# A gated expert mixture on one core: the moving columns of its matrix products laid out in alternating 16-byte runs

## The chip, the core and the metric
The kernel runs on one core of one Trainium2 chip. The metric is the device time of one execution in microseconds (us), median of several. The names of the engines: PE is TensorE, the matrix engine (PEld: its weight loads), DVE is VectorE, ACT is ScalarE, POOL is GpSimd, SP is SyncE, which issues the DMAs.

## The reference, cut to what matters
`x` has 16 sequences of 128 rows and 128 columns, float32. There are 8 routed experts and a shared one, each with a gate and an up projection 128 -> 512 and a down projection 512 -> 128.

```python
g = jnp.einsum('bsd,edf->ebsf', h, Wg)
u = jnp.einsum('bsd,edf->ebsf', h, Wu)
expert_outs = jnp.einsum('ebsf,efd->ebsd', jax.nn.silu(g) * u, Wd)
expert_output = jnp.einsum('be,ebsd->bsd', gating_probs, expert_outs)
shared = jnp.einsum('bsf,fd->bsd', jax.nn.silu(h @ Sg) * (h @ Su), Sd)
x = x + (1.0 - sg) * expert_output + sg * shared
x = x + jnp.einsum('bij,bjk->bik', T[itok - 1], x)
```

## The kernel before, in words
Everything is held transposed: 128 features on the partitions, (sequence, row) pairs as columns. The 2048 columns are four x tiles of W = 512 columns (NT = 4, four sequences each); the 512 hidden features are four chunks of 128 (NC = 4). A *unit* is one expert, one x tile and one chunk: 16 units to an expert, 9 experts, N = 144 units. Per unit PE makes three products, each as three matrix products of 128x128 weights with 512 moving columns. The split in three is for precision: every float32 operand is rounded to the type fp32r (`x_hi`, `w_hi`, `h_hi`) and the remainder kept as a second such operand (`x_lo`, `w_lo`, `h_lo`); hi*hi, hi*lo and lo*hi are added up in a PSUM bank.

Nine matrix products per unit, then: `project_g` (L444 to L446, the helper `product`) into `g_bank`, `project_u` (the same lines) into one of four `u_bank`, and `project_down` of the unit two before (LAG = 2), L470, L471 and L473, into `o_bank`, summed over the four chunks. The moving operands are `x_hi`/`x_lo` tile t for g and u, and `h_hi`/`h_lo` slot k % 4 (HR = 4 slots) for down.

Around them, per unit n:
- ACT: `silu` (L278) of g_bank into silu_g, and `round_h` of unit n - 1 (L284), which writes `h_hi` from `u_bank`.
- DVE: `make_h` (L342), u_bank times silu_g in place, and `split_h` of unit n - 1 (L348), which writes `h_lo` = u_bank - h_hi. Every fourth unit also `scale_group` (L356), o_bank times the routing coefficient.
- POOL: `acc` += scaled (L260) every fourth unit, and rounding and splitting the next expert's weights (`split_chunk`, L217 and L212). Each engine has its instructions in the order of its program; the waits are semaphores. `project_down` waits for `h_rounded` ahead of L470 and for `split_done` ahead of L473; `project_g` for `g_read`; `project_u` for `split_done` of four units before.
- SP: the weights of the expert after next, three DMAs of 256 KB; later the 16 matrices T and the results.

Before the loop the x tiles are written once: tile 0 by ACT (L307, `x_hi`) and DVE (L385, `x_lo`) from `o_bank`, which stands on the way to the first products (L510, L512, L514, then `project_u(0, 0)`, and L518 for the second unit's g); tiles 1 to 3 by `round_x` on ACT (L294) and `split_x` on POOL (L233). The semaphore `acc_done` holds PE at the first unit of each x tile of the first expert until `x_lo` is there.

Behind the last expert's units come the step matrices: `turn_y` (L483, transposes) and `step_y` (L491, plain float32 products of 128 columns, eight records for four sequences), copies on ACT (L289) and DVE (L371), and the stores. Two stretches of them lie between units; the last lies at the end. Their operands aren't touched by the change.

The straight layout of before is this: `x_hi` is `[P, NT, W]`, a tile's 512 columns lie one behind the other, and a moving operand is `x_hi[:, t, :]`, likewise `h_hi[:, slot, :]`.

Of the kernel before, what the change touches and what calls it, by code (L numbers as in the profile page):

```python
# [5 lines left out]
P = 128  # L6
F32 = mybir.dt.float32
F32R = mybir.dt.float32r
# [4 lines left out]
def moe_then_step_kernel(  # L13
# [32 lines left out]
    NT = B // BT  # L46
    W = BT * S
# [7 lines left out]
    EARLY = 3  # L55
    Q = 32
    assert NC == 4 and NT == 4 and E % 2 == 0

    with ExitStack() as ctx:
# [8 lines left out]
        zero = sb("zero", [P, P])  # L68
        x_hi = sb("x_hi", [P, NT, W], F32R)
        x_lo = sb("x_lo", [P, NT, W], F32R)  # L70
        w_raw = sb("w_raw", [P, 2, NC, 3, P])
        w_hi = sb("w_hi", [P, 2, NC, 3, P], F32R)
        w_lo = sb("w_lo", [P, 2, NC, 3, P], F32R)
        silu_g = sb("silu_g", [P, 2, W])
        h_hi = sb("h_hi", [P, HR, W], F32R)
        h_lo = sb("h_lo", [P, HR, W], F32R)
        scaled = sb("scaled", [P, 2, W])
# [15 lines left out]
        u_bank = [ctx.enter_context(nc.psum_tensor(f"u_bank{i}", [P, W], F32)) for i in range(HR)]  # L93
        o_bank = [ctx.enter_context(nc.psum_tensor(f"o_bank{i}", [P, W], F32)) for i in range(2)]

        x_in = [sem(f"x_in{i}") for i in range(3)]
# [107 lines left out]
        def _(pool):  # L204
# [25 lines left out]
            def split_x(t):  # L230

                pool.wait_ge(x_rounded, t + 1)
                nc.gpsimd.tensor_tensor(x_lo[:, t, :], acc[:, t, :], x_hi[:, t, :].bitcast(F32),  # L233
                                        ALU.subtract).then_inc(acc_done, 1)
# [38 lines left out]
        def _(act):  # L273
# [6 lines left out]
            def round_h(n, k):  # L280


                act.wait_ge(h_done, n + 1)
                nc.scalar.activation(h_hi[:, k % HR, :], u_bank[k % HR][:, :], ACT.Copy).then_inc(h_rounded, 1)  # L284

# [6 lines left out]
            def round_x(t):  # L292
                act.wait_ge(x_turned, t)
                nc.scalar.activation(x_hi[:, t, :], acc[:, t, :], ACT.Copy).then_inc(x_rounded, 1)  # L294

# [10 lines left out]
            act.wait_ge(x0_turned, 1)  # L306
            nc.scalar.activation(x_hi[:, 0, :], o_bank[0][:, :], ACT.Copy).then_inc(x_rounded, 1)  # L307
            act.wait_ge(w0_in, 32)
# [28 lines left out]
        def _(dve):  # L337
# [7 lines left out]
            def split_h(n, k):  # L345

                dve.wait_ge(h_rounded, n + 1)
                nc.vector.tensor_tensor(h_lo[:, k % HR, :], u_bank[k % HR][:, :], h_hi[:, k % HR, :].bitcast(F32),  # L348
                                        ALU.subtract).then_inc(split_done, 1)
# [29 lines left out]
            for m in range(2):  # L379
# [4 lines left out]
            dve.wait_ge(x_rounded, 1)  # L384
            nc.vector.tensor_tensor(x_lo[:, 0, :], o_bank[0][:, :], x_hi[:, 0, :].bitcast(F32),  # L385
                                    ALU.subtract).then_inc(split_done, 1)
# [54 lines left out]
        def _(pe):  # L441
# [6 lines left out]
            def project_g(n, k):  # L448

                t, c = k % U // NC, k % NC  # L450

                pe.wait_ge(g_read, n - 1)
                product(g_bank[k % 2][:, :], (k // U % 2, c, 0), x_hi[:, t, :], x_lo[:, t, :],
                        True, True).then_inc(g_done, 1)

            def project_u(n, k):
                t, c = k % U // NC, k % NC
                if k >= LAG:

                    pe.wait_ge(split_done, EARLY + n + 1 - HR)  # L460
                product(u_bank[k % HR][:, :], (k // U % 2, c, 1), x_hi[:, t, :], x_lo[:, t, :],
                        True, True).then_inc(u_done, 1)

            def project_down(n, k):

                t, c, slot = k % U // NC, k % NC, k % HR
                w = (k // U % 2, c, 2)

                pe.wait_ge(h_rounded, n + 1)
                nc.tensor.matmul(o_bank[t % 2][:, :], w_hi[:, w[0], w[1], w[2], :], h_hi[:, slot, :], start=c == 0, stop=False)  # L470
                nc.tensor.matmul(o_bank[t % 2][:, :], w_lo[:, w[0], w[1], w[2], :], h_hi[:, slot, :], start=False, stop=False)  # L471
                pe.wait_ge(split_done, EARLY + n + 1)
                last = nc.tensor.matmul(o_bank[t % 2][:, :], w_hi[:, w[0], w[1], w[2], :], h_lo[:, slot, :],  # L473
                                        start=False, stop=c == NC - 1)
                if c == NC - 1:
                    last.then_inc(o_done, 1)
# [32 lines left out]
            pe.wait_ge(x_rounded, 1)  # L509
            nc.tensor.matmul(g_bank[0][:, :], w_hi[:, 0, 0, 0, :], x_hi[:, 0, :], start=True, stop=False)  # L510
            pe.wait_ge(split_done, 1)
            nc.tensor.matmul(g_bank[0][:, :], w_lo[:, 0, 0, 0, :], x_hi[:, 0, :], start=False, stop=False)  # L512
            pe.wait_ge(split_done, EARLY)
            nc.tensor.matmul(g_bank[0][:, :], w_hi[:, 0, 0, 0, :], x_lo[:, 0, :], start=False, stop=True).then_inc(g_done, 1)  # L514
            project_u(0, 0)

            pe.wait_ge(w_ready, 1)
            product(g_bank[1][:, :], (0, 1, 0), x_hi[:, 0, :], x_lo[:, 0, :], True, True).then_inc(g_done, 1)  # L518
            project_u(1, 1)
# [58 lines left out]
```

## Time and profile before

| | us |
|---|---|
| time, median of 2 runs | 311.86 (311.65 to 312.06) |
| the profiled execution's own time | 312.09 |
| its span, first to last instruction | 310.1 |
| PE busy | 305.5 (99% of the span) |
| DVE busy | 217.5 (70%) |
| ACT busy | 164.6 (53%) |
| POOL busy | 102.2 (33%) |

The profile is that of one execution. A group of instructions is one line of the kernel with its operation, the tiles it writes and reads, and its shape; behind the count stand the busy time, the mean of one in ns, and the idle time of its engine just before, with what ended it. Matrix products are pipelined: a product's listed duration reaches past the start of the next, so rates are read from start to start. Start times are us from the span's start.

### The profile page before, as it was taken

To read this page: it belongs to the slowest core of one execution; us is meant where nothing else is said; L and a number is where in the kernel's file an instruction comes from. 1 tells how busy PE (TensorE), PEld (TensorE's weight loads), DVE (VectorE), ACT (ScalarE), POOL (GpSimd) and SP (SyncE) were. 2 spreads that over 40 slices of the span, in tenths; PEclk is the share of its full clock that TensorE was granted. 3 is DMA by queue.
4 is the path that set the end of the run, shared out by engine and by line. 5 is a ranking of instruction groups with operands and counts; after the bars stand their busy time and mean duration, and the time that the engine had idled before them with its cause. 6 is when DMAs were issued, how large, how long until landed. Compare 5 with 4: busy or idle time off the path is not lost.

```text
span 310.1 us, 4762 instructions
## 1 busy us (share of the span) xinstructions
PE 305.5 (99%) x1364; PEld 253.3 (82%) x1364; DVE 217.5 (70%) x355; ACT 164.6 (53%) x306; POOL 102.2 (33%) x116
## 2 busy tenths in 40 slices
PE   8999999999999999999999999999999999999996
PEld 7688888888888888888888888888888888888885
DVE  2786667766676666776667766677666766668885
ACT  5565555555555555555555555555555555555552
POOL 2565312441155115511552134411441155111310
PEclk9999999999999999999999999999999999999999
DMA  6930300030001100030003001100013000000112
GB/s 159 201 89 2 103 1 2 0 94 7 1 0 45 56 0 0 0 101 0 0 0 109 13 13 17 17 14 13 15 17 110 0 0 0 0 2 0 34 36 68
DMA packets 32727, 10.39 MB, mean 34 GB/s; under 512 B 16208, under 2 KB 32720, under 8 KB 32720
## 3 DMA queue, kind: packets, MB, share of 16 engines
q1 hardware_dynamic: 32720, 10.30, 13.5%
q8 instruction: 4, 0.07, 0.1%
q14 instruction: 3, 0.02, 0.0%
HBM read 9.25 MB, written 1.05 MB: 33 GB/s over the span
## 4 chain that ended last, share of the span: by engine, by line
PE 95%; SPq 1%; DMA 1%; POOL 0%; DVE 0%; ACT 0%; issue 0%
PE o_bank L470 11%; PE o_bank L473 11%; PE o_bank L471 11%; PE g_bank L446 10%; PE u_bank L446 10%; PE g_bank L445 10%; PE u_bank L445 10%; PE g_bank L444 10%; PE u_bank L444 10%; DMA w_raw<-in_L_cond_Wd 1%; PE o_bank L491 1%; SPq L158 1%; PE o_bank L483 0%; POOL w_lo L212 0%; DVE res L371 0%; PE u_bank L483 0%
## 5 line engine op out<-in xcount | busy, mean ns | idle before, releaser
L342 DVE TENSOR_TENSOR u_bank<-u_bank,silu_g 128x512 f32<-128x512 f32 x144 | 100.7, 699 | 84.2 <-PE u_bank L446 82.6
L278 ACT ACTIVATE silu_g<-g_bank 128x512 f32<-128x512 f32 x144 | 86.1, 598 | 132.8 <-PE g_bank L446 132.4
L348 DVE TENSOR_TENSOR h_lo<-u_bank,h_hi 128x512 fp32r<-128x512 f32 x144 | 97.9, 680 | 0.1
L260 POOL TENSOR_TENSOR acc<-acc,scaled 128x512 f32<-128x512 f32 x32 | 41.5, 1296 | 163.2 <-DVE scaled L356 163.0
L284 ACT ACTIVATE h_hi<-u_bank 128x512 fp32r<-128x512 f32 x144 | 85.4, 593 | 0.7 <-DVE u_bank L342 0.7
L470 PE MATMUL o_bank<-h_hi,w_hi 128*128 128x512 f32 x144 | 56.2, 390 | 0.8 <-POOL w_lo L212 0.8
L444 PE MATMUL u_bank<-x_hi,w_hi 128*128 128x512 f32 x144 | 56.1, 390 | 0.0
L473 PE MATMUL o_bank<-h_lo,w_hi 128*128 128x512 f32 x144 | 56.0, 389 | 0.0
L445 PE MATMUL u_bank<-x_lo,w_hi 128*128 128x512 f32 x144 | 56.0, 389 | 0.0
L471 PE MATMUL o_bank<-h_hi,w_lo 128*128 128x512 f32 x144 | 56.0, 389 | 0.0
L446 PE MATMUL u_bank<-x_hi,w_lo 128*128 128x512 f32 x144 | 56.0, 389 | 0.0
L444 PE MATMUL g_bank<-x_hi,w_hi 128*128 128x512 f32 x143 | 56.0, 392 | 0.0
L445 PE MATMUL g_bank<-x_lo,w_hi 128*128 128x512 f32 x143 | 55.7, 389 | 0.0
L446 PE MATMUL g_bank<-x_hi,w_lo 128*128 128x512 f32 x143 | 55.6, 389 | 0.0
L212 POOL TENSOR_TENSOR w_lo<-w_raw,w_hi 128x384 fp32r<-128x384 f32 (+2 forms) x36 | 35.8, 998 | 9.1 <-ACT w_hi L297 6.5
L470 PEld LDWEIGHTS o_bank<-h_hi,w_hi 128*128 128x128 f32 x144 | 27.0, 188 | 6.7 <-POOL w_lo L212 1.2
L445 PEld LDWEIGHTS u_bank<-x_lo,w_hi 128*128 128x128 f32 x144 | 27.1, 188 | 5.7
L444 PEld LDWEIGHTS u_bank<-x_hi,w_hi 128*128 128x128 f32 x144 | 27.2, 189 | 5.6
L473 PEld LDWEIGHTS o_bank<-h_lo,w_hi 128*128 128x128 f32 x144 | 27.0, 188 | 5.7 <-DVE h_lo L348 0.2
L471 PEld LDWEIGHTS o_bank<-h_hi,w_lo 128*128 128x128 f32 x144 | 27.0, 188 | 5.6
L446 PEld LDWEIGHTS u_bank<-x_hi,w_lo 128*128 128x128 f32 x144 | 27.0, 188 | 5.6
L446 PEld LDWEIGHTS g_bank<-x_hi,w_lo 128*128 128x128 f32 x143 | 26.8, 188 | 5.5
(49 smaller groups left out, 151.2 us busy)
## 6 DMA issues: line engine op xcount, KB each, us to landing
w_raw<-in_L_cond_Wd SPq DMA_DIRECT2D x8, 256.0 KB, 3.9
w_raw<-in_L_cond_Wg SPq DMA_DIRECT2D x7, 256.0 KB, 3.1
w_raw<-in_L_cond_Wu SPq DMA_DIRECT2D x7, 256.0 KB, 3.8
T_blk<-in_L_cond_T SPq DMA_DIRECT2D x64, 16.0 KB, 1.6
out_y<-res SPq DMA_DIRECT2D x3, 256.0 KB, 2.3
x_blk<-in_x SPq DMA_DIRECT2D x4, 128.0 KB, 3.6
x_nat<-in_x SPq DMA_DIRECT2D x1, 256.0 KB, 2.8
x_blk<-in_x SPq DMA_DIRECT2D x4, 64.0 KB, 2.7
```

Of the source, the lines that this page charges most:

```text
L212: return nc.gpsimd.tensor_tensor(w_lo[:, slot, c, m, :], w_raw[:, slot, c, m, :], w_hi[:, slot, c, m, :].bitcast(F32), ALU.subtract)
L260: nc.gpsimd.tensor_tensor(acc[:, t, :], acc[:, t, :], scaled[:, t % 2, :], ALU.add).then_inc(acc_done, 1)
L278: nc.scalar.activation(silu_g[:, k % 2, :], g_bank[k % 2][:, :], ACT.Silu).then_inc(g_read, 1)
L284: nc.scalar.activation(h_hi[:, k % HR, :], u_bank[k % HR][:, :], ACT.Copy).then_inc(h_rounded, 1)
L342: nc.vector.tensor_tensor(u_bank[k % HR][:, :], u_bank[k % HR][:, :], silu_g[:, k % 2, :], ALU.mult).then_inc(h_done, 1)
L348: nc.vector.tensor_tensor(h_lo[:, k % HR, :], u_bank[k % HR][:, :], h_hi[:, k % HR, :].bitcast(F32), ALU.subtract).then_inc(split_done, 1)
L444: nc.tensor.matmul(bank, w_hi[:, w[0], w[1], w[2], :], x_h, start=start, stop=False)
L445: nc.tensor.matmul(bank, w_hi[:, w[0], w[1], w[2], :], x_l, start=False, stop=False)
L446: return nc.tensor.matmul(bank, w_lo[:, w[0], w[1], w[2], :], x_h, start=False, stop=stop)
L470: nc.tensor.matmul(o_bank[t % 2][:, :], w_hi[:, w[0], w[1], w[2], :], h_hi[:, slot, :], start=c == 0, stop=False)
L471: nc.tensor.matmul(o_bank[t % 2][:, :], w_lo[:, w[0], w[1], w[2], :], h_hi[:, slot, :], start=False, stop=False)
L473: last = nc.tensor.matmul(o_bank[t % 2][:, :], w_hi[:, w[0], w[1], w[2], :], h_lo[:, slot, :], start=False, stop=c == NC - 1)
```

## The change
The tiles `x_hi`, `x_lo`, `h_hi` and `h_lo` get rows of 528 floats instead of 512 (ROW = W + 16), and a tile's columns are stored in another order. Logical column l*8 + h*4 + e (l from 0 to 63, h 0 or 1, e 0 to 3) lies at position h*256 + l*4 + e behind the tile's offset: runs of four floats (16 bytes) go alternately to the first and the second half. Where a form's second number is -1, l runs downwards: the last 16 bytes of each half come first. The offset within the row is 0, 8, 0, 8 floats for x tiles 0 to 3 and 4, 12, 4, 12 for h slots 0 to 3; tiles and slots 2 and 3 are the downward ones. Writers and readers use the same view, so that a matrix product's 512 result columns come out in their old order, and PSUM and all other tiles are read and written as before (`flat` only gives the same order the same dimensions). The order of instructions, their waits and counts stay.

```diff
+    ROW = W + 16
+    X_FORM = [(0, 1), (8, 1), (0, -1), (8, -1)]
+    H_FORM = [(4, 1), (12, 1), (4, -1), (12, -1)]
...
-        x_hi = sb("x_hi", [P, NT, W], F32R)
-        x_lo = sb("x_lo", [P, NT, W], F32R)
+        x_hi = sb("x_hi", [P, NT, ROW], F32R)
+        x_lo = sb("x_lo", [P, NT, ROW], F32R)
...
-        h_hi = sb("h_hi", [P, HR, W], F32R)
-        h_lo = sb("h_lo", [P, HR, W], F32R)
+        h_hi = sb("h_hi", [P, HR, ROW], F32R)
+        h_lo = sb("h_lo", [P, HR, ROW], F32R)
...
+        def woven(a, i, form):
+            at, way = form[i]
+            v = a[:, i, at:at + W].rearrange("p (h l e) -> p l h e", h=2, e=4)
+            return v[:, ::way, :, :]
+
+        def X(a, t):
+            return woven(a, t, X_FORM)
+
+        def H(a, slot):
+            return woven(a, slot, H_FORM)
+
+        def flat(v):
+            return v.rearrange("p (l h e) -> p l h e", h=2, e=4)
...
-                nc.gpsimd.tensor_tensor(x_lo[:, t, :], acc[:, t, :], x_hi[:, t, :].bitcast(F32),
+                nc.gpsimd.tensor_tensor(X(x_lo, t), flat(acc[:, t, :]), X(x_hi, t).bitcast(F32),
...
-                nc.scalar.activation(h_hi[:, k % HR, :], u_bank[k % HR][:, :], ACT.Copy).then_inc(h_rounded, 1)
+                nc.scalar.activation(H(h_hi, k % HR), flat(u_bank[k % HR][:, :]), ACT.Copy).then_inc(h_rounded, 1)
...
-                nc.scalar.activation(x_hi[:, t, :], acc[:, t, :], ACT.Copy).then_inc(x_rounded, 1)
+                nc.scalar.activation(X(x_hi, t), flat(acc[:, t, :]), ACT.Copy).then_inc(x_rounded, 1)
...
-                nc.vector.tensor_tensor(h_lo[:, k % HR, :], u_bank[k % HR][:, :], h_hi[:, k % HR, :].bitcast(F32),
+                nc.vector.tensor_tensor(H(h_lo, k % HR), flat(u_bank[k % HR][:, :]), H(h_hi, k % HR).bitcast(F32),
...
-                product(g_bank[k % 2][:, :], (k // U % 2, c, 0), x_hi[:, t, :], x_lo[:, t, :],
+                product(g_bank[k % 2][:, :], (k // U % 2, c, 0), X(x_hi, t), X(x_lo, t),
...
-                product(u_bank[k % HR][:, :], (k // U % 2, c, 1), x_hi[:, t, :], x_lo[:, t, :],
+                product(u_bank[k % HR][:, :], (k // U % 2, c, 1), X(x_hi, t), X(x_lo, t),
...
-                nc.tensor.matmul(o_bank[t % 2][:, :], w_hi[:, w[0], w[1], w[2], :], h_hi[:, slot, :], start=c == 0, stop=False)
-                nc.tensor.matmul(o_bank[t % 2][:, :], w_lo[:, w[0], w[1], w[2], :], h_hi[:, slot, :], start=False, stop=False)
+                nc.tensor.matmul(o_bank[t % 2][:, :], w_hi[:, w[0], w[1], w[2], :], H(h_hi, slot), start=c == 0, stop=False)
+                nc.tensor.matmul(o_bank[t % 2][:, :], w_lo[:, w[0], w[1], w[2], :], H(h_hi, slot), start=False, stop=False)
...
-                last = nc.tensor.matmul(o_bank[t % 2][:, :], w_hi[:, w[0], w[1], w[2], :], h_lo[:, slot, :],
+                last = nc.tensor.matmul(o_bank[t % 2][:, :], w_hi[:, w[0], w[1], w[2], :], H(h_lo, slot),
```

The first products (L510 to L514, L518), L307 and L385 change in the same way.

## Rows read from the trace of the kernel before
**Rows 1.** The page: busy time and share, granted TensorE clock in 40 slices.
```profile
PE 305.5 (99%) x1364; PEld 253.3 (82%) x1364; DVE 217.5 (70%) x355; ACT 164.6 (53%) x306; POOL 102.2 (33%) x116
...
PEclk9999999999999999999999999999999999999999
```
**Rows 2.** The page: the chain that ended last, by engine and line.
```profile
PE 95%; SPq 1%; DMA 1%; POOL 0%; DVE 0%; ACT 0%; issue 0%
PE o_bank L470 11%; PE o_bank L473 11%; PE o_bank L471 11%; PE g_bank L446 10%; PE u_bank L446 10%; PE g_bank L445 10%; PE u_bank L445 10%; PE g_bank L444 10%; PE u_bank L444 10%; DMA w_raw<-in_L_cond_Wd 1%; PE o_bank L491 1%; SPq L158 1%; PE o_bank L483 0%; POOL w_lo L212 0%; DVE res L371 0%; PE u_bank L483 0%
```
**Rows 3.** Groups by line, shapes kept apart: busy us, mean ns, idle before.
```profile
L342 DVE TENSOR_TENSOR u_bank<-u_bank,silu_g 128x512 f32<-128x512 f32 x144 | 100.7, 699 | 84.2 <-PE u_bank L446 82.6 <-ACT silu_g L278 1.4
L348 DVE TENSOR_TENSOR h_lo<-u_bank,h_hi 128x512 fp32r<-128x512 f32 x144 | 97.9, 680 | 0.1
L278 ACT ACTIVATE silu_g<-g_bank 128x512 f32<-128x512 f32 x144 | 86.1, 598 | 132.8 <-PE g_bank L446 132.4 <-PE g_bank L514 0.3
L284 ACT ACTIVATE h_hi<-u_bank 128x512 fp32r<-128x512 f32 x144 | 85.4, 593 | 0.7 <-DVE u_bank L342 0.7
L470 PE MATMUL o_bank<-h_hi,w_hi 128*128 128x512 f32 x144 | 56.2, 390 | 0.8 <-POOL w_lo L212 0.8
L444 PE MATMUL u_bank<-x_hi,w_hi 128*128 128x512 f32 x144 | 56.1, 390 | 0.0
...
L356 DVE TENSOR_TENSOR scaled<-o_bank,coef 128x512 f32<-128x512 f32 x32 | 21.7, 680 | 0.0
```
**Rows 4.** Timeline, 150.2 to 155 us, all engines: start us, duration us, instruction.
```profile
150.33 0.39 PE L470 MATMUL o_bank<-h_hi,w_hi 128*128 128x512 f32 x1
...
150.55 0.39 PE L471 MATMUL o_bank<-h_hi,w_lo 128*128 128x512 f32 x1
...
152.37 0.39 PE L470 MATMUL o_bank<-h_hi,w_hi 128*128 128x512 f32 x1
152.37 0.19 PEld L471 LDWEIGHTS o_bank<-h_hi,w_lo 128*128 128x128 f32 x1
152.38 0.59 ACT L284 ACTIVATE h_hi<-u_bank 128x512 fp32r<-128x512 f32 x1
...
153.24 0.68 DVE L348 TENSOR_TENSOR h_lo<-u_bank,h_hi 128x512 fp32r<-128x512 f32 x1
...
154.41 0.39 PE L470 MATMUL o_bank<-h_hi,w_hi 128*128 128x512 f32 x1
...
154.86 0.39 PE L473 MATMUL o_bank<-h_lo,w_hi 128*128 128x512 f32 x1
```
**Rows 5.** Timeline of PE: the first products of units 4 and 133.
```profile
16.37 0.39 PE L444 MATMUL g_bank<-x_hi,w_hi 128*128 128x512 f32 x1
...
279.53 0.39 PE L444 MATMUL g_bank<-x_hi,w_hi 128*128 128x512 f32 x1
```
**Rows 6.** Timeline of the start, 4.9 to 7.4 us.
```profile
4.96 0.58 ACT L307 ACTIVATE x_hi<-o_bank 128x512 fp32r<-128x512 f32 x1
...
5.58 0.69 DVE L385 TENSOR_TENSOR x_lo<-o_bank,x_hi 128x512 fp32r<-128x512 f32 x1 [0.20 <-ACT x_hi L307]
...
6.19 0.63 PE L512 MATMUL g_bank<-x_hi,w_lo 128*128 128x512 f32 x1
...
6.61 0.63 PE L514 MATMUL g_bank<-x_lo,w_hi 128*128 128x512 f32 x1
...
7.04 0.47 PE L444 MATMUL u_bank<-x_hi,w_hi 128*128 128x512 f32 x1
```
**Rows 7.** Timeline of PE near the end, 301.9 to 307.3 us.
```profile
303.37 0.40 PE L471 MATMUL o_bank<-h_hi,w_lo 128*128 128x512 f32 x1
303.60 0.40 PE L473 MATMUL o_bank<-h_lo,w_hi 128*128 128x512 f32 x1
303.84 0.40 PE L470 MATMUL o_bank<-h_hi,w_hi 128*128 128x512 f32 x1
304.07 0.39 PE L471 MATMUL o_bank<-h_hi,w_lo 128*128 128x512 f32 x1
304.30 0.39 PE L473 MATMUL o_bank<-h_lo,w_hi 128*128 128x512 f32 x1
304.53 1.05 PE L491 MATMUL o_bank<-y,T_plus 128*128 128x128 f32 x8
305.42 0.82 PE L483 MATMUL u_bank<-ident,yT 128*128 128x128 f32 x4
```
**Rows 8.** Timeline of POOL, 6 to 40 us.
```profile
6.58 2.13 POOL L212 TENSOR_TENSOR w_lo<-w_raw,w_hi 128x256 fp32r<-128x256 f32 x3 [5.10 <-ACT w_hi L297]
...
11.60 1.30 POOL L233 TENSOR_TENSOR x_lo<-acc,x_hi 128x512 fp32r<-128x512 f32 x1 [0.21 <-ACT x_hi L294]
...
13.76 0.42 POOL L242 TENSOR_TENSOR coef<-route_b,rest_b 128x128 f32<-128x128 f32 x1
16.89 1.29 POOL L233 TENSOR_TENSOR x_lo<-acc,x_hi 128x512 fp32r<-128x512 f32 x1 [2.71 <-ACT x_hi L294]
18.93 1.30 POOL L233 TENSOR_TENSOR x_lo<-acc,x_hi 128x512 fp32r<-128x512 f32 x1 [0.74 <-ACT x_hi L294]
```

More of the change, by code:

```diff
@@ L306, in _ @@
             act.wait_ge(x0_turned, 1)
-            nc.scalar.activation(x_hi[:, 0, :], o_bank[0][:, :], ACT.Copy).then_inc(x_rounded, 1)
+            nc.scalar.activation(X(x_hi, 0), flat(o_bank[0][:, :]), ACT.Copy).then_inc(x_rounded, 1)
             act.wait_ge(w0_in, 32)
@@ L384, in _ @@
             dve.wait_ge(x_rounded, 1)
-            nc.vector.tensor_tensor(x_lo[:, 0, :], o_bank[0][:, :], x_hi[:, 0, :].bitcast(F32),
+            nc.vector.tensor_tensor(X(x_lo, 0), flat(o_bank[0][:, :]), X(x_hi, 0).bitcast(F32),
                                     ALU.subtract).then_inc(split_done, 1)
@@ L509, in _ @@
             pe.wait_ge(x_rounded, 1)
-            nc.tensor.matmul(g_bank[0][:, :], w_hi[:, 0, 0, 0, :], x_hi[:, 0, :], start=True, stop=False)
+            nc.tensor.matmul(g_bank[0][:, :], w_hi[:, 0, 0, 0, :], X(x_hi, 0), start=True, stop=False)
             pe.wait_ge(split_done, 1)
-            nc.tensor.matmul(g_bank[0][:, :], w_lo[:, 0, 0, 0, :], x_hi[:, 0, :], start=False, stop=False)
+            nc.tensor.matmul(g_bank[0][:, :], w_lo[:, 0, 0, 0, :], X(x_hi, 0), start=False, stop=False)
             pe.wait_ge(split_done, EARLY)
-            nc.tensor.matmul(g_bank[0][:, :], w_hi[:, 0, 0, 0, :], x_lo[:, 0, :], start=False, stop=True).then_inc(g_done, 1)
+            nc.tensor.matmul(g_bank[0][:, :], w_hi[:, 0, 0, 0, :], X(x_lo, 0), start=False, stop=True).then_inc(g_done, 1)
             project_u(0, 0)
             pe.wait_ge(w_ready, 1)
-            product(g_bank[1][:, :], (0, 1, 0), x_hi[:, 0, :], x_lo[:, 0, :], True, True).then_inc(g_done, 1)
+            product(g_bank[1][:, :], (0, 1, 0), X(x_hi, 0), X(x_lo, 0), True, True).then_inc(g_done, 1)
             project_u(1, 1)
```

## The prediction
> **What bounds the kernel now.** I read the page's busy shares first. The matrix engine (PE) is busy 99% of the 310.1 us span, VectorE (DVE) 70%, ScalarE (ACT) 53%, GpSimd (POOL) 33% [rows 1]. The chain that ended last is 95% PE, spread evenly, 10 to 11% each, over the nine lines of matrix products [rows 2]. The reader is to see that in the loop no other engine's line stands in that chain. The groups by line say the same from the other side: silu waits 132.8 us in total for PE and the product on DVE waits 84.2 us, while PE's six kinds of product in the groups shown have next to no idle time before them [rows 3]. So the time is the number of products times their distance from start to start.
>
> That distance needs the timeline, since the durations overlap: each product is listed with 0.39 us, but the next starts 0.22 or 0.23 us later [rows 4]. From L470 at 150.33 to L470 at 152.37 lie nine products, 2.04 us, so 226.7 ns each. It hardly moves over the run: the group-opening L444 at 16.37 and the L444 at 279.53 are 129 units of nine products apart (units 4 and 133), and 263.16 us / 1161 = 226.7 ns again [rows 5]. 144 units x 9 = 1296 such products x 226.7 ns = 293.8 us of the 310.1.
>
> Is 226.7 ns the least that 512 columns need? At the start the engine still runs slow: L512 at 6.19, L514 at 6.61, L444 at 7.04 are 0.42 and 0.43 us apart [rows 6]. 512 columns at the lower of the two clock levels, 1.2 GHz, are 426.7 ns, and that is all the time these take. At the upper level, which the page grants throughout the loop [rows 1], the columns alone are 213.3 ns, and the trace shows 226.7. So 13.3 ns of each product, one part in sixteen, appear only at the upper clock. A fixed hand-over that isn't hidden would be seen at both. What fits is a supply of columns that cannot quite keep up with 2.4 GHz. There is a second sign: behind the transposes near the end, the starts 303.37, 303.60, 303.84, 304.07, 304.30, 304.53 are (304.53 - 303.37) / 5 = 232 ns apart, the same shape, same tiles and nobody waited for [rows 7]. The distance is therefore not a constant of the instruction; something in the streaming moves it by a few ns. Nothing in the trace says whether that something hangs on the addresses of the moving columns, and this is the whole question of the change.
>
> By the Trainium skill (TensorE: Matmul & The Clock Gate, "Wait — 56ns, not 53.3ns?"), back-to-back products start N / 1.2 GHz apart when the array is slow and N / 2.4 GHz plus about 2.5 ns when it is fast, 215.7 ns for N = 512. The slow half agrees with this trace (0.42 to 0.43 us); the fast half doesn't, by 11 ns. That page's figure is for 2-byte operands; these moving columns are 4 bytes. By it the sum below would be 226.7 - 215.7 = 11.0 ns x 1293 = 14.2 us.
>
> **The change part by part.**
> No instruction is added, removed or moved, no wait changes, and no DMA. Six kinds of instruction get another address pattern on one side: the products L444 to L446, L470, L471, L473 (and L510 to L514, L518) read their columns in runs of four floats, alternately from the two halves of a tile; round_h, split_h, round_x and split_x write them so. Tiles grow from 512 to 528 floats.
>
> *Products on PE.* All but three of the 1296 run at the upper clock (L510, L512 and L514 don't): 1293. Where two halves alternate, each half is asked for a run of 16 bytes every second run only. If the 13.3 ns come from runs that follow too closely in one place, this is the pattern that relieves it, and the different starts and directions keep x tiles and h tiles from meeting in the same phase. Ends: the whole 13.3 ns go, 13.3 x 1293 = 17.2 us; or they stay, 0; or the jump itself costs, and the loss is bounded below only by the nearest rate in the rows: one array cycle at 2.4 GHz, 0.42 ns, for each of 128 runs is 53.3 ns, 53.3 x 1293 = 68.9 us lost. I don't expect the full 13.3 to go, since something of each hand-over surely stays. What I have for it is the shorter products of the tail: eight products of 128 columns (two passes) at 304.53 to the next line at 305.42 are 111 ns apart for 106.7 ns of columns, so 4.6 ns, and I take 3.3 of the 13.3 as staying, nearer to the small column counts' 4.6 than to nothing. Term: 10.0 ns x 1293 = 12.9 us gained.
>
> *split_h on DVE.* Now 680 ns [rows 3]. No row shows runs of four; L356 writes four runs of 128 through a broadcast and takes 680 as well, so dimensions as such cost nothing there [rows 3]. Value 0; ends: 0 and doubled (+680 ns), a guess of size without a row, and a gain is excluded since the element count stays. Its cover: split_h of the unit whose g and u end at 150.33 runs 153.24 to 153.92, and the product that needs it, L473, starts at 154.86 [rows 4], 0.94 us later. Its throughput: in four units, 4 x 2.04 = 8.16 us, DVE does 4 x 0.70 + 4 x 0.68 + 0.68 = 6.20 us. It becomes the bound at (8.16 - 0.68 - 2.80) / 4 = 1.17 us per split_h. With units of 9 x 216.7 = 1.95 us that point is 1.08 us and the load 6.20 of 7.80.
>
> *round_h on ACT.* 593 ns [rows 3]. Value 0, up to doubled. silu and round_h are 1.19 of 2.04 us; doubled, 1.78, still below 1.95. For its own lateness: it ends 152.38 + 0.59 = 152.97, L470 needs it at 154.41 [rows 4], 1.44 us. Hidden even when doubled, though DVE's split_h then starts some 0.3 us later, out of its 0.94.
>
> *Prologue.* round_x(0) on ACT (0.58, at 4.96) and split_x(0) on DVE (0.69, at 5.58) stand before the first products [rows 6] and nothing covers them. Value 0; doubled both, +1.3 us. split_x(1) on POOL, 11.60 to 12.90, is needed by L444 at 16.37 [rows 5, 8], 3.5 us of cover; the other two start at 16.89 and 18.93 and are needed at 24.5 (8.16 us after 16.37) and 32.7. POOL's price for short runs: L242 writes 128 elements out of order in 0.42 us, no worse than the straight 128x256 of L212 at 0.71 (2.13 / 3) for twice as many [rows 8]. Hidden.
>
> *Larger tiles.* 64 bytes a tile more; no instruction works on them. 0.
>
> **Sum.** Against the profiled execution, 312.09 us: 312.09 - 12.9 = 299.2. The median shown is 311.86, 0.2 lower, so 299.0. If 10 ns go, a weight load, 0.19 us [rows 4] and started at once with the product before it, still ends before the next start 216.7 ns later.
>
> **The rivals.**
> A. *The columns' addresses don't matter at this grain.* For: every loop product takes 226.7 ns, whether x or h, whichever tile [rows 4, 5]; the writers come and go beside them without moving it. An excess due to addresses that meet would be expected to vary. It may be a limit on bytes per time, or come from the weight load beside it, which the change leaves alone. Against: the 232 ns of [rows 7]. Time: 311.9. Here also every relief or loss below 4.8 ns a product (2% of 311.9 us is 6.2 us; / 1293), which stays within about what a measurement of this kernel can tell from no change.
> The Trainium skill (SBUF — State Buffer, the paragraph on cachelines) has lines of 16 bytes, full rate while at least two accesses hit a line, and a price for crossing. Both the straight and the woven pattern hit each line four times and cross 128 times, so by this rule nothing changes and this rival's 311.9 results. Its price per crossing would fit the existence of 13.3 ns; no run here shows the line.
>
> B. *The jump costs PE.* One mechanism: whatever fetches columns ahead works on neighbours, and a run of 16 bytes is too short for it; downward tiles would be the worst. Place: each of 128 jumps of each of 1293 products, all on the chain. Price: the present 13.3 ns over 128 runs is 0.10 ns each; if each doubles, +17.2 us, 329; at one array cycle each, 312 + 69 = 381. It decides from 4.8 ns a product, 0.04 ns a jump. For: the present excess shows that the supply has no reserve at 2.4 GHz. Against: no row shows a pattern with such runs. I take 329 as its time.
>
> C. *DVE becomes the bound.* If split_h doubles to 1.36 us: 4 x 0.70 + 4 x 1.36 + 0.68 = 8.92 us against 8.16, 0.76 x 36 groups = 27 us, 339. It needs over 1.17 us. For: DVE reads one operand and writes the other in the new order. Against: L356's 680 ns.
>
> **How the numbers follow.** Forecast 299.0 with 0.44; A 0.32; B 0.20; C 0.04. The rate-only excess and its change behind the transposes speak for the forecast; its evenness speaks for A; nothing excludes B. The forecast's own range is 294.7 (all 13.3 ns gone) to 305.6 (4.8 ns gone). For 8 in 10: 295 at the lower end leaves out hardly anything, and upwards it takes in A whole and the small half of B; 322 leaves out the rest of B with C, some 0.18. Faster 0.44, within 2% 0.32, slower 0.24.
>
> **What would show it.** Right: L444 to L473 around 217 ns apart with durations near 0.38 instead of 0.39, a unit of 1.95 us, PE still 98 to 99% busy, DVE, ACT and POOL durations unchanged, shares of DVE and ACT up by 4 to 5%. If A: units of 2.04 us. If B: durations of products over 0.39 in woven lines and not in L491. If C: L348 over 1.17 us and PE waiting for h_lo. It would also be partly wrong if tiles of one form gain and those of another don't; then the distance differs between the x lines and the h lines, or between upward and downward tiles.

## The result and the profile after
The changed kernel takes 343.48 us (median of 2 runs, 343.45 to 343.50) against 311.86 us: 1.101 times the time of before, 95% interval 1.097 to 1.106. Forecast were 299.0 us and a range of 295 to 322. The profiled execution took 343.50 us, with a span of 341.3 us.

The page after: busy shares and granted clock (they answer to [rows 1]), then the chain that ended last, by engine and line ([rows 2]).

```profile
PE 337.4 (99%) x1364; PEld 256.1 (75%) x1364; DVE 217.8 (64%) x355; ACT 165.3 (48%) x306; POOL 102.2 (30%) x116
...
PEclk9999999999999999999999999999999999999999
...
PE 99%; DVE 0%; issue 0%
```

The work of DVE, ACT and POOL hasn't changed: 217.8, 165.3 and 102.2 us against 217.5, 164.6 and 102.2. The number of instructions and the clock are the same. PE alone is busy 32 us longer. The groups by line of the page after ([rows 3]; busy us, mean ns, idle before) say where:

```profile
L359 DVE TENSOR_TENSOR u_bank<-u_bank,silu_g 128x512 f32<-128x512 f32 x144 | 100.7, 700 | 114.9 <-PE u_bank L463 114.1
L295 ACT ACTIVATE silu_g<-g_bank 128x512 f32<-128x512 f32 x144 | 87.0, 605 | 163.4 <-PE g_bank L463 163.3
...
L365 DVE TENSOR_TENSOR h_lo<-u_bank,h_hi 128x512 fp32r<-128x512 f32 x144 | 98.0, 681 | 0.1
L301 ACT ACTIVATE h_hi<-u_bank 128x512 fp32r<-128x512 f32 x144 | 85.4, 593 | 0.7 <-DVE u_bank L359 0.7
...
L487 PE MATMUL o_bank<-h_hi,w_hi 128*128 128x512 f32 x144 | 59.9, 416 | 0.0
...
L461 PE MATMUL u_bank<-x_hi,w_hi 128*128 128x512 f32 x144 | 59.8, 415 | 0.0
```

The writers of the woven tiles cost what they did: split_h (L365) 681 ns against 680, round_h (L301) 593 against 593. They wait longer for PE. The products are listed with 415 ns instead of 390. From start to start, in PE's timeline of the kernel after, the first product of a unit is L461 on g_bank and a unit later it comes again; these two are 129 units apart ([rows 5]):

```profile
16.24 0.42 PE L461 MATMUL g_bank<-x_hi,w_hi 128*128 128x512 f32 x1
...
308.45 0.41 PE L461 MATMUL g_bank<-x_hi,w_hi 128*128 128x512 f32 x1
```

(308.45 - 16.24) / 1161 = 251.7 ns, against 226.7. So 25.0 ns x 1293 = 32.3 us. At the start 0.8 us is given back: the first down product waits for w_lo from 10.51 + 0.25 to 10.85 where it waited, before, until 11.45; that wait [rows 3, L470] belongs to a DMA that landed earlier in this execution. 32.3 - 0.8 = 31.5; the two spans differ by 31.2.

One more view, PE's timeline at the start of the kernel after, answers to [rows 6]. L529 and L531 are followed by the next product at the slow distance, L461 by one at the fast distance:

```profile
6.12 0.63 PE L529 MATMUL g_bank<-x_hi,w_lo 128*128 128x512 f32 x1
6.55 0.59 PE L531 MATMUL g_bank<-x_lo,w_hi 128*128 128x512 f32 x1
6.98 0.41 PE L461 MATMUL u_bank<-x_hi,w_hi 128*128 128x512 f32 x1
7.23 0.42 PE L462 MATMUL u_bank<-x_lo,w_hi 128*128 128x512 f32 x1
```

Woven columns are read here too, and yet the first starts are 0.43 us apart, just what 512 columns take at 1.2 GHz (426.7 ns). That the clock is the lower one here is read from this distance alone: the profile's granted clock is 1.00 in this stretch as well. At 2.4 GHz, where the columns alone are 213 ns, the same products are 0.25 us apart. In these two distances, then, the weave costs nothing at half the column rate.

### The profile page after: what moved, and what is told of

Read it like the earlier page. It is cut to its first block, busy times and chain, and to the rows that moved or that the text cites. A ratio compares the mean times of both kernels' runs of the same rounds, so it can differ in the third digit from the quotient of the medians.

```text
span 341.3 us, 4762 instructions
## 1 busy us (share of the span) xinstructions
PE 337.4 (99%) x1364; PEld 256.1 (75%) x1364; DVE 217.8 (64%) x355; ACT 165.3 (48%) x306; POOL 102.2 (30%) x116
## 4 chain that ended last, share of the span: by engine, by line
PE 99%; DVE 0%; issue 0%
PE u_bank L463 11%; PE g_bank L462 11%; PE o_bank L487 11%; PE o_bank L490 11%; PE u_bank L461 11%; PE u_bank L462 11%; PE g_bank L461 11%; PE o_bank L488 11%; PE g_bank L463 11%; PE o_bank L515 1%; PE o_bank L508 1%; PE o_bank L500 0%; DVE res L388 0%; PE o_bank L522 0%; PE u_bank L500 0%; PE g_bank L527 0%
## 5 line engine op out<-in xcount | busy, mean ns | idle before, releaser
L295 ACT ACTIVATE silu_g<-g_bank 128x512 f32<-128x512 f32 x144 | 87.0, 605 | 163.4 <-PE g_bank L463 163.3
L365 DVE TENSOR_TENSOR h_lo<-u_bank,h_hi 128x512 fp32r<-128x512 f32 x144 | 98.0, 681 | 0.1
L301 ACT ACTIVATE h_hi<-u_bank 128x512 fp32r<-128x512 f32 x144 | 85.4, 593 | 0.7 <-DVE u_bank L359 0.7
L463 PE MATMUL u_bank<-x_hi,w_lo 128*128 128x512 f32 x144 | 60.1, 417 | 0.0
L490 PE MATMUL o_bank<-h_lo,w_hi 128*128 128x512 f32 x144 | 59.9, 416 | 0.0
L487 PE MATMUL o_bank<-h_hi,w_hi 128*128 128x512 f32 x144 | 59.9, 416 | 0.0
L461 PE MATMUL g_bank<-x_hi,w_hi 128*128 128x512 f32 x143 | 59.9, 419 | 0.0
L462 PE MATMUL g_bank<-x_lo,w_hi 128*128 128x512 f32 x143 | 59.8, 418 | 0.0
L461 PE MATMUL u_bank<-x_hi,w_hi 128*128 128x512 f32 x144 | 59.8, 415 | 0.0
L462 PE MATMUL u_bank<-x_lo,w_hi 128*128 128x512 f32 x144 | 59.8, 415 | 0.0
L488 PE MATMUL o_bank<-h_hi,w_lo 128*128 128x512 f32 x144 | 59.5, 413 | 0.0
L463 PE MATMUL g_bank<-x_hi,w_lo 128*128 128x512 f32 x143 | 59.4, 415 | 0.0
L461 PEld LDWEIGHTS u_bank<-x_hi,w_hi 128*128 128x128 f32 x144 | 27.5, 191 | 9.2
```

What stands on the lines that cost most here:

```text
L295: nc.scalar.activation(silu_g[:, k % 2, :], g_bank[k % 2][:, :], ACT.Silu).then_inc(g_read, 1)
L301: nc.scalar.activation(H(h_hi, k % HR), flat(u_bank[k % HR][:, :]), ACT.Copy).then_inc(h_rounded, 1)
L365: nc.vector.tensor_tensor(H(h_lo, k % HR), flat(u_bank[k % HR][:, :]), H(h_hi, k % HR).bitcast(F32), ALU.subtract).then_inc(split_done, 1)
L461: nc.tensor.matmul(bank, w_hi[:, w[0], w[1], w[2], :], x_h, start=start, stop=False)
L462: nc.tensor.matmul(bank, w_hi[:, w[0], w[1], w[2], :], x_l, start=False, stop=False)
L463: return nc.tensor.matmul(bank, w_lo[:, w[0], w[1], w[2], :], x_h, start=False, stop=stop)
```

## The experiments
Theory at this point: PE's reading of the woven columns costs, by its jumps. Rivals: directions and offsets; the woven writes of other engines; the weight load beside each product; the number of dimensions of the pattern. Each experiment is one execution, except for the one taken again in rounds; the kernel before, run beside them, took 311.4 to 312.6 us, so a difference of 1 us says nothing.

### Series of products by themselves
Three questions can be put to PE alone. This kernel is the one before with series of 24 products behind its end, each series on a line of its own:

```diff
+            F = x_hi[:, :, :].rearrange("p t w -> p (t w)")
...
+            pe.wait_ge(g_read, N)
...
+            for _ in range(24):  # straight
+                nc.tensor.matmul(g_bank[0][:, :], w_hi[:, 0, 0, 0, :], F[:, 0:512], start=True, stop=True)
+            for _ in range(24):  # woven_up
+                nc.tensor.matmul(g_bank[0][:, :], w_hi[:, 0, 0, 0, :], weave(F[:, 0:512], 4), start=True, stop=True)
...
```

> The kernel before, with 24 warm-up products and then 18 series of 24 products of 128x512 behind the end of PE's work, other engines idle, one weight tile, one source line per address pattern of the moving columns. Theory 'other engines': with nobody else at SBUF, straight columns fall below 226.7 ns per product and woven ones (251.5 ns in the changed kernel) come within 3 ns of them. Theory 'each jump to a non-neighbouring 16-byte run costs': straight 226.7, woven upward and downward about 251, runs of 8 floats about 239, of 16 floats 233, of 64 floats 228, runs of 2 at 276 or more; gaps between runs of 4 cost like the weave; one 16-byte line read over and over, without a jump to another line, at most 226.7. Theory 'the inner loop of the address pattern costs, wherever it points': runs of 4 that repeat one line, and runs of 4 that go downwards side by side, cost about 251 as well.

PE's timeline of it, each series merged to a row; the distance of the products is the next row's start less this one's, divided by 24:

```profile
312.11 5.60 PE L566 MATMUL g_bank<-x_hi,w_hi 128*128 128x512 f32 x24
317.55 5.72 PE L568 MATMUL g_bank<-x_hi,w_hi 128*128 128x512 f32 x24
323.11 5.77 PE L570 MATMUL g_bank<-x_hi,w_hi 128*128 128x512 f32 x24
328.71 6.18 PE L572 MATMUL g_bank<-x_hi,w_hi 128*128 128x512 f32 x24
334.73 6.11 PE L574 MATMUL g_bank<-x_hi,w_hi 128*128 128x512 f32 x24
340.67 8.16 PE L576 MATMUL g_bank<-x_hi,w_hi 128*128 128x512 f32 x24
348.66 6.01 PE L578 MATMUL g_bank<-x_hi,w_hi 128*128 128x512 f32 x24
354.51 5.92 PE L580 MATMUL g_bank<-x_hi,w_hi 128*128 128x512 f32 x24
360.27 5.63 PE L582 MATMUL g_bank<-x_hi,w_hi 128*128 128x512 f32 x24
365.73 5.71 PE L584 MATMUL g_bank<-x_hi,w_hi 128*128 128x512 f32 x24
371.28 5.92 PE L586 MATMUL g_bank<-x_hi,w_hi 128*128 128x512 f32 x24
377.04 5.77 PE L588 MATMUL g_bank<-x_hi,w_hi 128*128 128x512 f32 x24
382.64 5.76 PE L590 MATMUL g_bank<-x_hi,w_hi 128*128 128x512 f32 x24
388.24 6.16 PE L592 MATMUL g_bank<-x_hi,w_hi 128*128 128x512 f32 x24
...
406.31 5.41 PE L598 MATMUL g_bank<-x_hi,w_hi 128*128 128x512 f32 x24
411.55 11.10 PE L600 MATMUL g_bank<-x_hi,w_hi 128*128 128x512 f32 x24
```

| line | moving columns | ns |
|---|---|---|
| L566 | straight | 226.7 |
| L568, L570 | straight, 16 and 32 bytes on | 231.7, 233.3 |
| L572, L574 | woven in runs of 4, up and down | 250.8, 247.5 |
| L576 | woven in runs of 2 | 332.9 |
| L578, L580, L582 | woven in runs of 8, 16, 64 | 243.8, 240.0, 227.5 |
| L584, L586 | runs of 4 (of 16), each followed by a gap as long | 231.3, 240.0 |
| L588, L590 | downwards, singly and in runs of 4 | 233.3, 233.3 |
| L598 | one 16-byte run 128 times | 218.3 |
| L600 | every second column | 455, mean of start distances |

The straight 226.7 and the woven 250.8 are both here with every other engine idle. That settles it: the other engines have no part in either. A jump to a run that is not a neighbour isn't what costs the 24 ns: L584 jumps 127 times and loses 4.6 ns, L590 loses 6.7. Nor is it the two-level pattern, which L598 has at 218.3. The loss isn't proportional to the number of jumps either: 16-float runs keep 13.3 of 24 ns with a quarter of the jumps, and runs of two floats lose 106, not twice 24. The expectation "each jump to a non-neighbouring 16-byte run costs" failed on all three counts. Every second column, contiguous runs given up altogether, takes twice the time of straight columns.

### The parts of the change in the kernel
Edits to the changed kernel, each by itself. The weave alone:

```diff
-    ROW = W + 16
-    X_FORM = [(0, 1), (8, 1), (0, -1), (8, -1)]
-    H_FORM = [(4, 1), (12, 1), (4, -1), (12, -1)]
+    ROW = W
+    X_FORM = [(0, 1)] * 4
+    H_FORM = [(0, 1)] * 4
```

> The changed kernel with the weave alone: all tiles upwards, no offsets, rows of 512 floats. Theory 'the weave itself costs': 341 to 346 us as the changed kernel, 251 ns a product. Rival 'direction and the tiles' own offsets cost': back near 312 us.

341.23 us, the kernel before on the same chip 312.26; its units are 2.25 us, 250.0 ns a product over 128 units. It was taken again in rounds:

> The weave alone (upwards, no offsets) again, timed in rounds: 341.2 us, which is 2.3 us less than the changed kernel's 343.5, so that directions and offsets carry less than a tenth of its loss of 31.6 us. Were they a real help against the weave's cost, the weave alone would be above 343.5.

341.25 us, ratio to before 1.095 (1.092 to 1.097). The weave carries 29.7 us of loss beside 311.56; directions, offsets and longer rows, in the changed kernel, the remaining 2 us or so.

The offsets and longer rows alone:

```diff
-            v = a[:, i, at:at + W].rearrange("p (h l e) -> p l h e", h=2, e=4)
-            return v[:, ::way, :, :]
+            return a[:, i, at:at + W]
...
```

> The changed kernel with straight, upward columns, but its rows of 528 floats and the offsets of 0, 8 and 4, 12 floats. Theory 'the weave itself costs': 312 us, 226.7 ns. Rival 'the tiles' own offsets cost': over 320 us. If offsets help, below 310 us.

319.08 us, 232.0 ns a product. I had expected nothing; offsets and rows of 2112 bytes together cost 6.8 us. (The longer rows move the tiles too: modulo 256 bytes, the x tiles start at 0, 96, 128 and 224, not only at 0 and 32.) With the weave in place they add next to nothing: the two losses (29.7 and 6.8) don't add up.

Directions alone (no weave, no offsets, rows of 512; tiles and slots 2 and 3 in runs of four downwards):

```diff
...
-            v = a[:, i, at:at + W].rearrange("p (h l e) -> p l h e", h=2, e=4)
-            return v[:, ::way, :, :]
+            v = a[:, i, 0:W].rearrange("p (l e) -> p l e", e=4)
+            return v[:, ::way, :]
...
```

> No weave and no offsets; tiles and slots 2 and 3 keep their columns in runs of four that go downwards, all others straight. From the series (233.3 against 226.7 ns for half of the products): 6.7 x 648 = 4.3 us, 316 us; if the change between directions disturbs the straight ones too (231 to 232), 319 us. If direction is free: 312.

317.49 us, 231.1 ns on average: downward tiles 233.6 to 233.8, straight ones 228.1 to 229.6, between the two expected cases. So each of the three parts (weave; offsets with longer rows; directions) is a loss alone.

Longer runs:

```diff
-            v = a[:, i, at:at + W].rearrange("p (h l e) -> p l h e", h=2, e=4)
+            v = a[:, i, at:at + W].rearrange("p (h l e) -> p l h e", h=2, e=16)
...
-            return v.rearrange("p (l h e) -> p l h e", h=2, e=4)
+            return v.rearrange("p (l h e) -> p l h e", h=2, e=16)
```

> The changed kernel with runs of 16 floats (64 bytes) instead of 4, offsets and directions kept. If each jump costs, 32 jumps instead of 128 leave a quarter of the 24.8 ns: 233 ns a product, about 320 us. If the pattern costs only by being in several dimensions, however long the run: 343 us. If offsets and direction cost: 343 us.

326.31 us, 237.7 ns. 11.0 ns x 1293 = 14.2 us; the difference is 14.1. Again not a quarter of the loss but over 40%; in the series it was over a half.

### Who takes part: writers, weights, column width
The woven writes alone, PE reading straight (in the version with the weave alone):

```diff
...
-                product(g_bank[k % 2][:, :], (k // U % 2, c, 0), X(x_hi, t), X(x_lo, t),
+                product(g_bank[k % 2][:, :], (k // U % 2, c, 0), x_hi[:, t, 0:W], x_lo[:, t, 0:W],
...
-                nc.tensor.matmul(o_bank[t % 2][:, :], w_hi[:, w[0], w[1], w[2], :], H(h_hi, slot), start=c == 0, stop=False)
+                nc.tensor.matmul(o_bank[t % 2][:, :], w_hi[:, w[0], w[1], w[2], :], h_hi[:, slot, 0:W], start=c == 0, stop=False)
...
```

> ACT, DVE and POOL write x and h tiles woven (upwards, no offsets), PE reads them straight, so the columns of g, u and o come out in another order than the reference's. If all the cost lies in PE's reading: 312 us, 226.7 ns a product. If the woven writes disturb PE's reading of SBUF: above 315 us.

312.43 us against 311.58 on the same chip, and 226.7 ns a product: the writes cost PE nothing. All of the loss is in PE's reading.

h tiles straight, x tiles woven (in the version with the weave alone):

```diff
         def H(a, slot):
-            return woven(a, slot, H_FORM)
+            return flat(a[:, slot, 0:W])
```

> x tiles woven upwards without offsets, h tiles straight for writers and PE. If the cost is per woven product and adds up, two thirds of the loss of the version with the weave alone (341.2 us against 312.3): 312.3 + 2/3 x 29 = 331.6 us, with down products at 226.7 to 232 ns. If it comes from one kind of tile meeting the other's writers, all or nothing of it.

335.01 us. PE's timeline of it: three down products with straight columns, then the first of g with woven ones.

```profile
149.92 0.40 PE L486 MATMUL o_bank<-h_hi,w_hi 128*128 128x512 f32 x1
150.16 0.40 PE L487 MATMUL o_bank<-h_hi,w_lo 128*128 128x512 f32 x1
150.39 0.39 PE L489 MATMUL o_bank<-h_lo,w_hi 128*128 128x512 f32 x1
150.62 0.41 PE L460 MATMUL g_bank<-x_hi,w_hi 128*128 128x512 f32 x1
```

(150.62 - 149.92) / 3 = 233 ns. The straight products between woven ones don't get back to 226.7, which is why the time lies above the 331.6 of the plain sum. A straight product reaches 226.7 only behind several straight, equally placed ones: the kernel before shows the same behind its transposes [rows 7], and in the series the first products after a change of pattern are off as well. The last series of p3, straight columns behind woven ones, has distances of 235, 233, 236, 224 and 231 ns before it settles at 227.

More series, for weights, dimensions and width (the same kind of diff as the first, with other operands):

> Again the kernel before with series of 24 products behind the end of PE's work. Theory 'the moving columns meet the weight load that runs beside them': with the weights read from one word over and over, straight columns fall from 226.7 to about 218 ns (the value of one repeated line) and woven ones from 250 to about 218 as well; and straight columns 16 bytes on, with the weights 16 bytes on too, are back at 226.7 from 231.5. Theory 'the moving stream's own jumps cost, whatever the weights do': with one-word weights woven columns stay near 250 and straight ones near 226. Theory 'the third dimension costs': three dimensions with small jumps cost 250, two dimensions with steps of 48 and 64 bytes stay near 231. Theory 'supply at 4 bytes a column': with 2-byte columns the straight series takes at most 217 ns and the woven one (16-byte runs) less than 5 ns more. A fixed cost per product would show as the same excess over 106.7 and 53.3 ns with 256 and 128 columns; a cost per run as a half and a quarter of 13 ns.

```profile
328.27 5.76 PE L578 MATMUL g_bank<-x_hi,w_hi 128*128 128x512 f32 x24
333.88 5.63 PE L580 MATMUL g_bank<-x_hi,w_hi 128*128 128x512 f32 x24
339.35 5.65 PE L582 MATMUL g_bank<-x_hi,w_hi 128*128 128x512 f32 x24
...
355.90 5.71 PE L588 MATMUL g_bank<-x_hi,w_hi 128*128 128x512 f32 x24
361.44 5.81 PE L590 MATMUL g_bank<-x_hi,w_hi 128*128 128x512 f32 x24
367.09 6.14 PE L592 MATMUL g_bank<-x_hi,w_hi 128*128 128x512 f32 x24
373.06 6.24 PE L594 MATMUL g_bank<-x_hi,w_hi 128*128 128x512 f32 x24
...
400.95 5.60 PE L604 MATMUL g_bank<-x_hi,w_hi 128*128 128x512 f32 x24
406.38 5.92 PE L606 MATMUL g_bank<-x_hi,w_hi 128*128 128x512 f32 x24
412.15 5.94 PE L608 MATMUL g_bank<-x_hi,w_hi 128*128 128x512 f32 x24
...
423.60 3.04 PE L612 MATMUL g_bank<-x_hi,w_hi 128*128 128x256 f32 x24
426.48 2.80 PE L614 MATMUL g_bank<-x_hi,w_hi 128*128 128x128 f32 x24
...
429.34 5.13 PE L616 MATMUL g_bank<-x_hi,w_hi 128*128 128x512 bf16 x23
434.30 5.34 PE L618 MATMUL g_bank<-x_hi,w_hi 128*128 128x512 bf16 x24
```

This is PE's timeline again. With the weights read from a single word, straight columns take 230.8 ns (L588) and woven ones 248.8 (L592); woven columns with weights 16 bytes on take 253 (L594). So the weave's loss is there wherever the weights lie. The weight load itself ran beside every product of every series; that it has a part in the loss is not excluded. The few ns of an offset do hang on the weights: straight columns take 233 ns when only the weights are moved by 32 bytes (L578), 233 when only the columns are (L570 of the first series), and 228 when both are (L580). At 16 bytes it is 227 with only the weights moved, 231 with only the columns and 230 with both, so no simple rule of equal places comes out. Three dimensions with small jumps (L604: 16-byte runs 0, 2, 5, 7, 10, 12 ...) take (406.38 - 400.95) / 24 = 226.3 ns, so three dimensions and small jumps cost nothing; the same three dimensions with a second half 1088 bytes away (L606) take 240.4. And 2-byte columns take 215.7 ns straight (L616, 23 of its products recorded) and, by the mean of their start distances in the trace, 215.8 woven in 16-byte runs (L618): no loss. 256 straight columns take 120.0 (L612), 13.3 over their 106.7, as many as 512 have. 128 columns don't fit: their starts are 109.5 ns apart on average, 56 over their 53.3. What bounds them stays open.

### Which distance of the halves
The helper builds pairs of 16-byte runs, the second d runs behind the first, the next pair s further on:

```diff
+            def pair(buf, d, s, r=64, at=0):
+                v = buf[:, at:at + 4]
+                a = list(v.ap)
+                return bass.AP(v.tensor, v.offset, [a[0], [4 * s, r], [4 * d, 2], [1, 4]])
```

> Series of 24 products behind the kernel before; the moving columns are pairs of 16-byte runs, the second d runs' length behind the first, the next pair s further on. Theory 'places that are used again too soon': d = 64, 128, 192, 256 (multiples of 64, as the weave's 1024 bytes) cost about 250 ns, d = 65 about 260, d = 66 and 67 less, d of 68 and more 240 or less; a pair at d = 64 whose next is 3 or 7 on still costs 250. Theory 'going far and back costs': all d from 64 to 256 cost alike, and small pairs (2, 3), (1, 3), (3, 4) stay near 227 to 231. Fixed or per column: if the weave's loss of some 23 ns is per run, 256 columns lose half of it (120 + 12 = 132 ns); if it is per product, 120 + 23 = 143. For 384 straight columns 160 + 13.3 = 173.3 if the straight excess is per product, 170 if it is per column.

> Series behind the kernel before, to see whether the distance of the two halves counts modulo 16 runs (256 bytes). If it does: d = 64, 80 about 250 ns, d = 65, 81 alike (about 251), d = 73, 74, 76, 88, 104, 136 alike with 72 (240 to 243), d = 63 like 79, d = 82 like 66 (243), d = 84 like 68 (242). If it is modulo 64 runs: 81, 82, 84 near 240. Steps of 2, 3, 4 and 5 runs with 384 columns: 2 to 4 within 5 ns of the straight 173.3; 5 at about 200 if the 266 ns found in another tile come from the step, 173 to 180 if they came from the tile. 2-byte columns (16-byte runs at step 5): 163 ns, no loss, if only the 4-byte rate has no reserve; 2-byte columns in runs of 8 bytes woven near 216 by the same; every second 2-byte column likewise near 216 if what counts is bytes per time, more if it is hits per 16 bytes.

PE's timeline of the second of the two (p4; the first is p3). L585 is d = 64, the weave of the change; L587 is 65, L599 is 81, L601 is 82, L607 is 104; L597 is 80.

```profile
318.29 6.17 PE L585 MATMUL g_bank<-x_hi,w_hi 128*128 128x512 f32 x24
324.30 6.39 PE L587 MATMUL g_bank<-x_hi,w_hi 128*128 128x512 f32 x24
330.52 5.93 PE L589 MATMUL g_bank<-x_hi,w_hi 128*128 128x512 f32 x24
...
353.80 6.18 PE L597 MATMUL g_bank<-x_hi,w_hi 128*128 128x512 f32 x24
359.81 6.39 PE L599 MATMUL g_bank<-x_hi,w_hi 128*128 128x512 f32 x24
366.03 6.00 PE L601 MATMUL g_bank<-x_hi,w_hi 128*128 128x512 f32 x24
...
383.45 5.92 PE L607 MATMUL g_bank<-x_hi,w_hi 128*128 128x512 f32 x24
389.21 5.92 PE L609 MATMUL g_bank<-x_hi,w_hi 128*128 128x512 f32 x24
```

| d, in 16-byte runs (s = 1) | ns, mean of start distances |
|---|---|
| 64, 80, 96, 128, 192, 256 | 250 |
| 65, 81 | 259 (65 once 251, in p3) |
| 66, 82 | 243 |
| 63, 79 | 243 |
| 68, 84 | 242 |
| 72, 88, 104, 136 | 240 |

Every pair of distances that are equal modulo 16 runs (256 bytes) costs the same: 64 and 80, 65 and 81 (within p4), 66 and 82, 68 and 84, 63 and 79, and the four of 72. What stands out is 0 and 1 modulo 16; all the others tried lie between 240 and 243. In p4, 80 is (359.81 - 353.80) / 24 = 250.4 and 104 is 240.0. With 256 woven columns the product takes 127.2 ns against 120.0 straight, with 384 it takes 191.5 against 173.7: 7, 18 and 24 ns for 256, 384 and 512 columns, so the weave's loss grows with the columns. The straight excess doesn't: 120.0, 173.7 and 226.7 are each 13 to 14 over their columns, of which one repeated run keeps 5.2 both at 256 (111.9) and 512 (218.5). But it isn't free of addresses: 256 straight columns that start 16 bytes on take 116.9.

The table holds for s = 1 and halves at their first place. In p3's timeline the same d = 64 with the next pair 48 bytes on (s = 3, L610) takes 267 ns, where its expectation had 250:

```profile
388.99 6.57 PE L610 MATMUL g_bank<-x_hi,w_hi 128*128 128x512 f32 x24
395.39 6.31 PE L612 MATMUL g_bank<-x_hi,w_hi 128*128 128x512 f32 x24
```

With s = 2 it takes 246, with s = 7, 256. d = 65 with s = 3 takes 234, and d = 41 with s = 7, 227.5. The weave of the change itself, begun 16, 32, 48 or 64 bytes on, takes 251, 247, 243 and 249.

The law isn't simple, and I can't give it. Uniform steps of 2, 3 and 4 runs take 173.2 to 173.5 ns with 384 columns, as straight ones do, but a step of 5 takes 199.9. With 512 columns, read from w_lo, a step of 5 takes 266 and one of 6 takes 320. 2-byte columns at that same step of 5 take 163.0, without any loss. But every second 2-byte column takes 225.9 where 215.8 is the contiguous value, and 2-byte columns woven in runs of 8 bytes take 226.7; near 216 was expected for both if only the 4-byte rate had no reserve.

In the kernel, against the version with the weave alone, halves 1088 bytes apart (d = 68):

```diff
-    ROW = W
+    ROW = W + 32
...
-            v = a[:, i, at:at + W].rearrange("p (h l e) -> p l h e", h=2, e=4)
-            return v[:, ::way, :, :]
+            v = a[:, i, 0:ROW].rearrange("p (h l e) -> p l h e", h=2, e=4)
+            return v[:, 0:64, :, :]
```

> The weave alone, upwards, no offsets, with the second half 1088 bytes behind the first instead of 1024. From the series of products (240.0 against 250 ns): 1293 x 10 = 13 us less than the weave alone at 341.2, so 328 us. If the distance of the halves doesn't matter in the kernel: 341.

330.32 us, 241.1 ns a product, against 341.25 with 1024 bytes. Moving the second half by 64 bytes gives back 10.9 us. The longer rows move tiles and slots 1 and 3 as well, to 128 bytes modulo 256: these take 240.0 ns, the others, in their old places, 242.2. So the distance of the halves alone gives 7.8 of the 250.0 ns back. In all, the addresses of the moving columns alone take this kernel anywhere from 312 to 343 us, and every departure tried in it from straight tiles at equal places was slower.

## Why the prediction was wrong
**What bounds the kernel.** Right: PE's distance from start to start sets the time, and it alone moved. The unit numbers of [rows 5] were one too low (they are units 5 and 134), which leaves the 226.7 ns as it was, but tile 1's x_lo is needed at 14.33, not 16.37; its cover on POOL was 1.4 us, not 3.5. It was enough: POOL's L250 after takes 1.30 us, as before.

**"What fits is a supply of columns that cannot quite keep up with 2.4 GHz."** Half right, and the half that was wrong carried the forecast. The address-dependent losses need a high rate: woven columns lose nothing at 1.2 GHz (two distances) and nothing with 2-byte columns in 16-byte runs; 2-byte columns in 8-byte runs lose 10.9 ns. But the straight 13.3 ns weren't such a loss per column: 256, 384 and 512 columns all have them. I excluded a fixed amount per product because it didn't show at the lower clock, and that doesn't follow: from 256 to 512 columns the series show an amount that is fixed per product, at the upper clock. What it consists of stays open. The 4.6 ns of the tail, from which I took the 3.3 that would stay, needn't say anything about it: a product of 128 columns takes 109.5 ns in p2 with 53.3 ns of columns, nearly the tail's 111.

**"If the 13.3 ns come from runs that follow too closely in one place, this is the pattern that relieves it."** This is the step that failed. The weave doesn't relieve anything. It alternates between places 1024 bytes apart, and with runs that follow one another in each half, all distances tried that are a multiple of 256 bytes cost 250 ns. Why they do stays open. The term was +10.0 ns x 1293 gained; measured, it is -25.0 ns x 1293. My ends were 13.3 gained and 53.3 lost, so the measured value lay within the bounds I had worked out, though not within the range that I stated: between rival B's first price (+13.3) and its end (+53.3).

**Rival B** was the right place and sign, with 0.20, and its two prices, 329 and 381 us, lie on both sides of 343. Its mechanism, the run of 16 bytes that is too short, is only in part what was found: runs of four at steps of 2, 3 or 4 runs are nearly free, in three dimensions too, while alternating halves cost by their distance. "Downward tiles would be the worst" was wrong: woven downwards is 247.5 against 250.8 upwards.

**Rival A.** Its evidence, 226.7 for x and h and every tile, was true and misread by me: all tiles start at places that are equal among themselves, so that evenness spoke neither for nor against a dependence on addresses. The 232 ns behind the transposes were the hint, though to something else: six products that had not settled yet, as at the end of p3. Offsets and longer rows bring the whole kernel to the same 232.0 ns (319.08 us). By the Trainium skill (SBUF — State Buffer, the paragraph on cachelines) at least two hits on a 16-byte line give full rate, and each crossing to a new line has a price. The series disagree: woven runs of four hit each line four times and cross as often as straight columns do, and take 250.8 ns against 226.7; every second column hits each line twice and takes 455, where 256 crossings would give 240 if the straight 13.3 ns were wholly the price of 128. The measurement decides.

**DVE, ACT, POOL and rival C.** Value 0, as forecast: 681, 593 and 1297 ns, and the writers' version takes 312.43 us. Larger tiles: not 0 as a part, since longer rows move the tiles; no run has them without offsets and without the weave.

**The 215.7 ns of 2-byte columns.** By the Trainium skill (TensorE: Matmul & The Clock Gate, "Wait — 56ns, not 53.3ns?") that is the distance at N = 512; with 2-byte columns the series gives 215.8, so the rule holds there. No 4-byte series reached it: the lowest with 512 columns is 218.5, and that only for one repeated run.

**The range** ended at 322 because I let the upper end cut off most of B. With a rival whose price had bounds from 0 to 69 us, it should have reached well beyond 329.

## What to carry to other kernels
When 4-byte moving columns stream at full clock, keep them contiguous and all tiles at like places, and don't pad or interleave them without measuring: 16 bytes of offset cost 2% per product, a second stream at a multiple of 256 bytes 10%, every second column 100%. An excess over the ideal rate isn't evidence that a rearrangement would lift it; 24 products at the end of a kernel on a line of their own answer that for any pattern, before anything is rebuilt. An interval that is the same in all rows tells nothing about a quantity that was the same in all rows too.

## What the runs showed of the hardware that I had not expected
- The time of a product with 4-byte moving columns depends on their addresses. Two alternating streams of contiguous 16-byte runs cost 250 ns a product at distances of 0, 259 at 16, 243 at 32 and 240 at 128 bytes (all modulo 256), against 226.7 straight. With other steps within the streams the same distances cost otherwise (234 to 267 ns). A uniform step of 80 bytes costs 26 ns in 384 columns; steps of 32, 48 and 64 none. Every second column doubles the time (455 ns).
- The dependence vanishes at half the column rate (0.43 us, two distances) and with 2-byte columns in 16-byte runs (215.8 ns), also at the step of 80 bytes. It doesn't with 2-byte columns in 8-byte runs (226.7) or with every second one (225.9).
- Where the weights lie counts for a few ns: moving either weights or columns by 32 bytes costs 6.6 ns, moving both about 1.
- The distance of one product depends on those before it. Straight columns settle at 226.7 ns only after several equally placed predecessors, and stay near 233 between woven ones.
- Other engines' traffic, heavy in the loop, doesn't move the distance at all: 226.7 straight both with it and without.
